# Attention probabilities leave two PSUM banks together: one instruction per engine and row, and waits per key block

## The reference

```
logits = einsum("bhqd,bhkd->bhqk", q, k) + causal + pos_bias
probs  = softmax(logits / 64)
out    = einsum("bhqk,bhkd->bhqd", probs, v)
x = x + layernorm(out_of_all_heads @ Wo + bo)
x = x + layernorm(moe(layernorm(x)))
```

## The kernel before

| slot | scores of row | transposes of row | fillers |
|---|---|---|---|
| 6 | 6 | 4 | values of the far half, key blocks 6 and 7 |
| 7 | 7 | 5 | values of the near half, block 0; the output projection in two pieces |
| 0 | 0 | 6 | values, near half, block 1; a q/k projection |
| 1 | 1 | 7 | values, near half, blocks 2 and 3; a q/k projection |
| 2 | 2 | 0 | none |
| 3 | 3 | 1 | values, far half, blocks 0 to 2; the output projection |
| 4, 5 | 4, 5 | 2, 3 | values, far half, block 3; then blocks 4 and 5 |

## Time and profile before

### The profile page before, as it was taken

The page is one execution under the profiler, slowest core; times in us unless marked ns, Lnnn a source line. Parts: engine busy times, 40 slices in busy tenths (PEclk is TensorE's granted clock), DMA queues, the critical chain, the costliest instruction groups (busy, mean ns, idle before and its releaser), DMA issues.

```text
span 858.1 us, 17060 instructions
## 1 busy us (share of the span) xinstructions
PE 770.3 (90%) x4436; PEld 656.1 (76%) x4436; DVE 712.8 (83%) x1596; ACT 612.1 (71%) x1340; POOL 298.6 (35%) x323
## 2 busy tenths in 40 slices
PE   3877999999999999999999999998469999999992
PEld 2657888888888888888888888887357877777771
DVE  5567888888888888888888888887879789998976
ACT  2356877877787788778777877875457776676672
POOL 2228723323332333233233323322321444554423
PEclk9999999999999999999999999999679999999997
DMA  7783244324423432443244234330003111222101
GB/s 274 242 267 81 62 85 89 72 61 86 98 61 72 93 80 61 86 93 66 61 92 92 61 76 89 79 74 26 25 1 126 48 39 61 73 73 73 50 1 49
DMA packets 56025, 70.72 MB, mean 82 GB/s; under 512 B 36032, under 2 KB 45120, under 8 KB 52544
## 3 DMA queue, kind: packets, MB, share of 16 engines
q1 hardware_dynamic: 55712, 69.83, 32.3%
q10 hardware_dynamic: 288, 0.59, 0.3%
HBM read 27.36 MB, written 9.50 MB: 43 GB/s over the span
## 4 chain that ended last, share of the span: by engine, by line
PE 70%; DVE 10%; issue 7%; ACT 5%; POOL 4%; DMA 3%; ACTq 0%; POOLq 0%; DVEq 0%; SPq 0%
PE out_ps L1184 16%; PE trans_ps L1166 15%; PE score_ps L1151 12%; PE shared_ps L1196 6%; DVE pT_lo L854 3%; PE trans_ps L1067 3%; PE score_ps L1067 2%; PE score_ps L1069 2%; ACT pT_hi L663 2%; PE score_ps L1068 2%; PE trans_ps L1068 2%; PE trans_ps L1069 2%; DVE pT_lo L954 2%; PE shared_ps L1067 2%; PE shared_ps L1069 2%
## 5 line engine op out<-in xcount | busy, mean ns | idle before, releaser
L648 ACT ACTIVATE probs<-score_ps,row_min 128x128 f32<-128x128 f32 (+7 forms) x256 | 190.3, 743 | 53.6 <-DVE row_min L841 53.0
L663 ACT ACTIVATE pT_hi<-trans_ps 128x512 fp32r<-128x512 f32 (+3 forms) x384 | 185.8, 493 | 58.6 <-PE out_ps L1184 30.0
L854 DVE TENSOR_TENSOR pT_lo<-trans_ps,pT_hi 128x512 fp32r<-128x512 f32 (+3 forms) x384 | 201.7, 553 | 30.4 <-ACT pT_hi L663 29.0
L841 DVE CUSTOM_DVE_ANT_0 score_ps<-score_ps,bias 128x128 f32<-128x128 f32 (+7 forms) x256 | 194.2, 759 | 20.9 <-PE score_ps L1151 18.9
L1166 PE MATMUL trans_ps<-ident,probs 128*128 128x128 f32 x1152 | 190.2, 274 | 20.7 <-DVE pT_lo L854 19.7
L1151 PE MATMUL score_ps<-k_hl,q_hl 128*128 128x512 f32 (+2 forms) x768 | 182.4, 351 | 3.2 <-DMA k_hl<-k_hl 1.6
L469 POOL TENSOR_TENSOR acc<-acc,head_out 128x512 f32<-128x512 f32 x64 | 82.8, 1294 | 263.1 <-DVE head_out L872 262.9
L1166 PEld LDWEIGHTS trans_ps<-ident,probs 128*128 128x128 f32 x1152 | 136.9, 140 | 44.8 <-DVE pT_lo L854 28.0
L1184 PE MATMUL out_ps<-pT_hi,v_hl 128*128 128x512 f32 (+2 forms) x384 | 156.5, 409 | 1.1 <-DVE pT_lo L854 1.1
L954 DVE TENSOR_TENSOR pT_lo<-probs,pT_hi 128x512 fp32r<-128x512 f32 x144 | 133.0, 950 | 25.0 <-ACT pT_hi L721 15.0
L1151 PEld LDWEIGHTS score_ps<-k_hl,q_hl 128*128 128x128 f32 x768 | 134.4, 188 | 23.7 <-DMA k_hl<-k_hl 1.8
(11 more groups left out here) (122 smaller groups left out, 1160.2 us busy)
## 6 DMA issues: line engine op xcount, KB each, us to landing
q_hl<-k_hl SPq DMA_DIRECT2D x64, 256.0 KB, 3.6
k_hl<-k_hl SPq DMA_DIRECT2D x32, 512.0 KB, 4.2
v_scratch<-probs SPq DMA_DIRECT2D x16, 512.0 KB, 4.1
v_raw<-v_scratch SPq DMA_DIRECT2D x32, 256.0 KB, 4.6
bias_all<-gate_scratch SPq DMA_DIRECT2D x8, 1024.0 KB, 4.8
v_raw<-in_Wfc SPq DMA_DIRECT2D x8, 256.0 KB, 4.9
bias<-in_Wproj SPq DMA_DIRECT2D x8, 256.0 KB, 5.3
bias_all<-in_rel_steps SPq DMA_DIRECT2D x1, 1920.0 KB, 12.8
```

The costliest lines, as they stand in the source:

```text
L648: act.activation(probs[s % 4][:, 0:n], scores_of(s % QB)[:, 0:n], ACT.Exp, bias=row_min[:, s:s + 1], scale=-1.0, accum_out=row_sum[:, s:s ...
L663: act.activation(pT_hi[c][:, CH * g:CH * g + m, q * P:(q + 1) * P], trans_ps[k % 2][:, 0:m * P].rearrange("p (m q) -> p m q", q=P), ACT.Co ...
L841: dve.tensor_tensor_reduce(out=ps, in0=ps, in1=bias_b[b][:, T - n:T], scale=1.0, scalar=3e38, op0=ALU.add, op1=ALU.min, accum_out=row_min[ ...
L854: dve.tensor_tensor(pT_lo[c][dst], trans_ps[k % 2][:, 0:m * P].rearrange("p (m q) -> p m q", q=P), pT_hi[c][dst], ALU.subtract).then_inc(p ...
```

## The change

`trans_ps` becomes two halves of one tile of 1024 columns over two banks. Rows of up to four blocks use bank i % 2. Rows of five blocks or more use both banks, and leave them in one instruction on ACT and one on DVE. `pT_psum`, `pT_hi_ready` and `pT_ready` now count rows (256), not groups (384). PE waits at a row's first group: for row 0 and rows 4 to 7 until all rows before are out; for rows 2 and 3 until the row two before is; for row 1 nothing more. The near half's wait on `oT_psum` stays. The far half's is split: its rows 4, 5 and 6 wait on a new semaphore `far_used`, which `values` raises after key blocks 3, 4, 5 and 6, and row 7 waits on `oT_psum`. The other edits write `trans_ps[r]` for `trans_ps[r][:]`.

```
+    def banks_of(i):
+        return [i % 2] if i < CH else [0, 1]
...
-        trans_ps = [pb(f"trans_ps{r}", [P, W]) for r in range(2)]
+        trans_wide = pb("trans_wide", [P, 2 * W])
+        trans_ps = [trans_wide[:, r * W:(r + 1) * W] for r in range(2)]
...
 split_hi (ACT)
-                if q == 0 and not (isinstance(u, int) and u < NC):
+                used = not (isinstance(u, int) and u < NC)
+                if c == 0 and q == 0 and used:
                     act.wait_ge(oT_psum, u - (NC - 1))
-                for g in range(GROUPS[i]):
-                    k = group_of(s, g)
-                    m = min(CH, i + 1 - CH * g)
-                    act.wait_ge(pT_psum, h * G_HEAD + k + 1)
-                    act.activation(pT_hi[c][:, CH * g:CH * g + m, q * P:(q + 1) * P],
-                                   trans_ps[k % 2][:, 0:m * P].rearrange("p (m q) -> p m q", q=P),
-                                   ACT.Copy).then_inc(pT_hi_ready, 1)
+                if c and used and q == CH - 1:
+                    act.wait_ge(oT_psum, u - (NC - 1))
+                elif c and used:
+                    act.wait_ge(far_used, (h * B + b - 1) * CH + q + 2)
+                act.wait_ge(pT_psum, h * S + s + 1)
+                at = banks_of(i)[0] * W
+                act.activation(pT_hi[c][:, 0:i + 1, q * P:(q + 1) * P],
+                               trans_wide[:, at:at + (i + 1) * P].rearrange("p (m q) -> p m q", q=P),
+                               ACT.Copy).then_inc(pT_hi_ready, 1)
...
 split_lo (DVE)
-                for g in range(GROUPS[i]):
-                    ...
-                    dve.wait_ge(pT_hi_ready, h * G_HEAD + k + 1)
-                    dve.tensor_tensor(pT_lo[c][dst], trans_ps[k % 2][:, 0:m * P]...
+                dve.wait_ge(pT_hi_ready, h * S + s + 1)
+                dve.tensor_tensor(pT_lo[c][dst], trans_wide[:, at:at + (i + 1) * P]...
...
 transpose_probs (PE)
                 if g == 0:
                     pe.wait_ge(probs_ready, h * S + s + 1)
-                if not (isinstance(h, int) and h == 0 and k < 2):
-                    pe.wait_ge(pT_ready, h * G_HEAD + k - 1)
+                    if i == 0 or i >= CH:
+                        if not (isinstance(h, int) and h == 0 and s == 0):
+                            pe.wait_ge(pT_ready, h * S + s)
+                    elif i > 1:
+                        pe.wait_ge(pT_ready, h * S + s - 1)
+                bank = banks_of(i)[g]
...
-                last.then_inc(pT_psum, 1)
+                if g == len(banks_of(i)) - 1:
+                    last.then_inc(pT_psum, 1)
...
 values (PE)
+                    if c and CH - 1 <= j < nk - 1:
+                        last.then_inc(far_used, 1)
```

More of the change, by code:

```diff
@@ L256, in transformer_block @@
         oT_psum = sem("oT_psum")
+        far_used = sem("far_used")
         oT_ready = sem("oT_ready")
@@ L602, in nT_evac @@
                 act.wait_ge(nT_psum, n * NCH + c + 1)
-                act.activation(nT_hi[:, c * W:(c + 1) * W], trans_ps[c % 2][:], ACT.Copy)\
+                act.activation(nT_hi[:, c * W:(c + 1) * W], trans_ps[c % 2], ACT.Copy)\
                    .then_inc(nT_hi_ready, 1)
@@ L791, in nT_evac @@
                 dve.wait_ge(nT_hi_ready, n * NCH + c + 1)
-                dve.tensor_tensor(nT_lo[:, c * W:(c + 1) * W], trans_ps[c % 2][:],
+                dve.tensor_tensor(nT_lo[:, c * W:(c + 1) * W], trans_ps[c % 2],
                                   nT_hi[:, c * W:(c + 1) * W], ALU.subtract).then_inc(nT_ready, 1)
@@ L848, in split_lo @@
                 c, q = divmod(i, CH)
-                for g in range(GROUPS[i]):
-                    k = group_of(s, g)
-                    m = min(CH, i + 1 - CH * g)
-                    dst = (slice(None), slice(CH * g, CH * g + m), slice(q * P, (q + 1) * P))
-                    dve.wait_ge(pT_hi_ready, h * G_HEAD + k + 1)
-                    dve.tensor_tensor(pT_lo[c][dst], trans_ps[k % 2][:, 0:m * P].rearrange("p (m q) -> p m q", q=P),
-                                      pT_hi[c][dst], ALU.subtract).then_inc(pT_ready, 1)
+                dst = (slice(None), slice(0, i + 1), slice(q * P, (q + 1) * P))
+                at = banks_of(i)[0] * W
+                dve.wait_ge(pT_hi_ready, h * S + s + 1)
+                dve.tensor_tensor(pT_lo[c][dst], trans_wide[:, at:at + (i + 1) * P].rearrange("p (m q) -> p m q", q=P),
+                                  pT_hi[c][dst], ALU.subtract).then_inc(pT_ready, 1)
             def invert_sums(h, b, c, j0, j1):
@@ L961, in gate_expert @@
                 if isinstance(e, int) and e == 0:
-                    dve.tensor_scalar(acc_T[:, cols], trans_ps[c % 2][:], bias, None, ALU.add)\
+                    dve.tensor_scalar(acc_T[:, cols], trans_ps[c % 2], bias, None, ALU.add)\
                        .then_inc(gated_ready, 1)
@@ L969, in gate_expert @@
                 dve.sem_inc(dve_passed, 1)
-                dve.scalar_tensor_tensor(out=gated[c % 2][:], in0=trans_ps[c % 2][:], scalar=bias,
+                dve.scalar_tensor_tensor(out=gated[c % 2][:], in0=trans_ps[c % 2], scalar=bias,
                                          in1=gate_rows[i][:, cols], op0=ALU.add, op1=ALU.mult)\
@@ L1158, in transpose_probs @@
                 i = s % QB
-                k = group_of(s, g)
                 if g == 0:
                     pe.wait_ge(probs_ready, h * S + s + 1)
-                if not (isinstance(h, int) and h == 0 and k < 2):
-                    pe.wait_ge(pT_ready, h * G_HEAD + k - 1)
+                    if i == 0 or i >= CH:
[4 more added lines that the diff above has]
+                bank = banks_of(i)[g]
                 for j in range(CH * g, min(CH * (g + 1), i + 1)):
                     o = (j - CH * g) * P
-                    last = pe.transpose(trans_ps[k % 2][:, o:o + P], probs[s % 4][:, j * P:(j + 1) * P], ident[:])
-                last.then_inc(pT_psum, 1)
+                    last = pe.transpose(trans_ps[bank][:, o:o + P], probs[s % 4][:, j * P:(j + 1) * P], ident[:])
+                if g == len(banks_of(i)) - 1:
+                    last.then_inc(pT_psum, 1)
             def values(h, b, c, j0, j1):
@@ L1173, in values @@
                 if j0 == 0:
-                    pe.wait_ge(pT_ready, h * G_HEAD + group_of(QB * b + CH * c + CH - 1, c) + 1)
+                    pe.wait_ge(pT_ready, h * S + QB * b + CH * c + CH)
                     if c == 0:
@@ L1225, in slot @@
                 if s >= LAG_PE or carried:
-                    for g in range(GROUPS[t % QB]):
+                    for g in range(len(banks_of(t % QB))):
                         transpose_probs(n, t, g)
@@ L1244, in _ @@
                 if s - LAG_PE < S:
-                    for g in range(GROUPS[(s - LAG_PE) % QB]):
+                    for g in range(len(banks_of((s - LAG_PE) % QB))):
                         transpose_probs(H - 1, s - LAG_PE, g)
@@ L1281, in second_layer @@
                 for k in range(HB):
-                    last = three(trans_ps[c % 2][:], wproj_hi[i][:, k, :], wproj_lo[i][:, k, :],
+                    last = three(trans_ps[c % 2], wproj_hi[i][:, k, :], wproj_lo[i][:, k, :],
                                  hidden_hi[c % 2][k], hidden_lo[c % 2][k], start=k == 0, stop=k == HB - 1)
```

## The result

The changed kernel takes **987.36 us** (985.56 to 988.69, 4 runs), the kernel before 861.41 (860.6 to 862.1). The ratio is 1.146 with a 95% interval of 1.1435 to 1.1487: slower by 126 us, where 118 were forecast. The profiled execution took 985.56 us over a span of 983.8, which is 125.6 more than the profiled execution before.

What follows compares the result with a forecast made beforehand. PE was taken to bound the kernel; losing the second buffer adds 3.70 us per unit, 118 us over 32 units, to the profiled 859.9, and with 1.1 for the median gives 979 us, range 950 to 1000.

Steps and rivals of the forecast that it cites:

- What bounds: Attention units: PE bounds, busy 16.2 of 16.8 us a unit, with one 0.56 us gap ahead of row 5's transposes.
- The three unguarded places: Ahead of the transposes of rows 6, 7 and the next row 0: no PE gap before the change; the ones to watch.
- The merged instructions: One ACT copy and one DVE subtraction per long row: 128 fewer on each engine, worth nothing on the path alone.
- The line through two forms: Merged instruction times from the 128 and 512 column forms: 105 ns per key block on ACT, 135 on DVE.
- bound on this price: Merged instructions' price per unit: 0.8 us less or 0.5 us more than the line, giving 953 to 996 us.
- The single buffer: PE's T0 of rows 5, 6, 7 and 0 waits for the whole row before: 3.70 us more per unit, 118 us.
- Row 4's new wait for row 3: Ahead of row 4's T0, PE must also wait for row 3 to leave; costed at nothing.
- the hand-over of 0.04 us from DVE to PE: From DVE's end to PE's next transposes: 0.04 us, part of 0.17 us of hand-overs per trip.
- row 4's gain of 0.04: After row 4's trip of 1.70 us, row 5's T0 would start at 318.72 instead of 318.76, 0.04 us earlier.
- The clock rival: Granted clock falls to 1.2 GHz from row 5 to row 0: 1104 us, chance 0.05; few units, near 1000, 0.03.
- hidden trips, faster: Trips of rows 5 to 7 fit behind PE's work, only row 5's wait counts: 19 us gained, 842 us, chance 0.02.
- What would show it: Profile signs: PE gaps ahead of rows 5, 6, 7, 0 of about 0.5, 1.0, 1.5, 1.2 us; wait some 130 us.

Runs made afterwards that it cites:

- e2_row_wait: Kernel before plus the waits per key block and PE's wait for the whole row before; instructions stay in pairs: 876.69 us, ratio 1.019.
- e4_act_merged: e1_block_wait with ACT's copy merged to one per row, DVE's subtractions in pairs, PE waiting by group: 932.17 us, ratio 1.083.
- e3_dve_merged: e2_row_wait with DVE's subtraction merged to one per row, ACT's copies still in pairs: 928.87 us, ratio 1.079.
- e1_block_wait: Kernel before with the far half's waits per key block alone; groups, banks and pairs of instructions stay: 843.38 us, ratio 0.980.
- e7_waits_swapped: Changed kernel with PE's two waits ahead of T0 exchanged, first pT_ready, then probs_ready: 982.01 us, ratio 1.140.

## Why the prediction was right

The sign, the place and the mechanism were as forecast, and 987.36 lies within 950 to 1000. Point by point:

- *What bounds.* The three unguarded places were the right ones to watch. All gained a gap.
- *The merged instructions.* The line through two forms held within 1% for all four lengths. Groups by form (count, busy us, mean ns, idle before):

```profile
L851 DVE TENSOR_TENSOR pT_lo<-trans_wide,pT_hi 128x1024 fp32r<-128x1024 f32 x32 | 39.2, 1225 | 52.1 <-ACT pT_hi L662 52.1
...
L662 ACT ACTIVATE pT_hi<-trans_wide 128x1024 fp32r<-128x1024 f32 x32 | 32.9, 1027 | 58.9 <-PE trans_wide L1166 58.9
```

  1.027 and 1.225 us against 1.022 and 1.230. Neither bound on this price (953 and 996) was needed. The Trainium skill, page "VectorE: DVE Perf Modes", section "The TRN2 errata — SBUF-src ops pay a fixed extra latency per instruction", was right about a fixed part per instruction, but the 20 us estimated from it did not show: the subtractions' own busy time fell by 8.0 us (201.7 to 193.7 by the two pages) and all of DVE's by 1.4. The pairs had already overlapped.
- *The single buffer.* Intervals forecast from rows 4, 5, 6 and 7: 2.64, 3.28, 3.52 and 3.77 us. Measured in the two units above: 2.78, 3.27, 3.56, 3.78 and 2.78, 3.34, 3.60, 3.83. Behind row 0 there were 7.28 us, where 7.2 and 0.06 for the late start were forecast. Row 4's new wait for row 3 cost nothing, as forecast: no gap stands ahead of it. The forecast did not single out that the merges, more than PE's wait, take the second buffer away; e2_row_wait and e4_act_merged show it.
- *The term that was mis-sized: the hand-over of 0.04 us from DVE to PE.* I took it from the one place where the trace of before had it. In the changed kernel's chain it is mostly 0.14. It also turned row 4's gain of 0.04 into a loss of 0.10. The long kind goes with the merged subtraction. From 150 to 560 us, all 25 hand-overs that PE waited for in the kernel before took about 0.06 us from DVE's end, and so did all 72 in e2_row_wait and all 85 in e4_act_merged, where DVE still subtracts in two halves. With one subtraction per row 75 of 86 in e3_dve_merged and 69 of 79 in the changed kernel took about 0.15. Why is not shown. At 0.09 us, three and a half times a unit, that is 10 us in 32 units, an estimate. Part of it was hidden by luck: the hand-over from PE to ACT, taken as 0.11, is only 0.08 behind rows 4 and 5, and 0.02 behind rows 6 and 7. The chain behind row 4's T1, which ends at 331.88:

```profile
331.88 0.02 issue
331.90 0.02 ACTq L660
331.92 0.04 issue
331.96 0.71 ACT pT_hi L662
```

  Per unit the average is 20.75 us against 20.51 forecast (16.81 and 3.70), 0.24 more, or 7.4 us over 31 units.
- *The clock rival came true in one place.* In the last unit the granted clock falls. Stretches of the changed kernel, and the transposes behind its three longest gaps in this part:

```profile
690.00:705.00 15.00, 11.02 (x74) 9.59 (x73) 8.94 (x22) 8.06 (x19) 2.58 (x2) 1.00 0.06 17
705.00:712.70 7.70, 5.21 (x36) 4.12 (x34) 4.69 (x8) 5.00 (x8) 1.40 (x2) 1.00 0.27 70
712.80:715.00 2.20, 1.05 (x5) 1.08 (x6) 1.00 (x1) 0.00 (x0) 0.20 (x1) 0.50 0.00 0
715.00:720.00 5.00, 3.42 (x13) 2.84 (x12) 2.92 (x11) 1.51 (x2) 0.00 (x0) 0.50 0.00 0
```
```profile
693.44 0.63 PE L1166 MATMUL trans_wide<-ident,probs 128*128 128x128 f32 x4 [2.05 <-DVE pT_lo L851]
...
697.28 0.30 PE L1166 MATMUL trans_wide<-ident,probs 128*128 128x128 f32 x1 [1.93 <-DVE pT_lo L851]
...
713.95 1.94 PE L1166 MATMUL trans_wide<-ident,probs 128*128 128x128 f32 x8 [1.93 <-DVE pT_lo L851]
```

  It goes from 2.4 to 1.2 GHz at 712.8 us, inside the gap of 1.93 us ahead of the last row 7, when PE had been idle for 0.7 us. The length of one gap does not tell when: the gaps of 2.05 and 1.93 us shortly before left the clock at 1.00, and so did those of up to 1.35 us from 100 to 690 us. The forecast named a granted clock under 1.00 in attention as a sign of being wrong; it shows, but only in the last 3 us of the transposes, where row 7's eight take 1.94 us instead of the 1.07 of the earlier trace rows. The last transposes begin 122.6 us later than before (715.5 against 592.9), and the rest of the 125.6, 3.0 us, falls behind them. There the first 7.1 us run at 0.50, and before the change they ran at 1.00; how much of the 3.0 us that is was not separated.
- *The rival "hidden trips, faster", 842 us*, was refuted for this change. Its gain is real, though: e1_block_wait takes it, 843.4 us, by leaving the merges out. The Trainium skill, page "TensorE: Matmul & The Clock Gate", section "HAM oscillation — how this bites in real kernels", reports no further gain from PSUM double-buffering in its kernel. Here e4_act_merged, which gives up little else, costs 89 us.
- *What would show it.* The gap ahead of row 5 was forecast at 0.5 and is 0.63; the others at 1.0, 1.5 and 1.2 and are 0.8, 1.3 and 1.2. A gap is counted from the modelled end of the last matmul, which can lie later than the next one's start would put it, and that may be why two are smaller. For the same reason, as I read it, PE's busy time rose from 770 to 788 us, which I had said would stay: the tail of a matmul that used to overlap the next one now stands alone ahead of each gap. The total wait was forecast at some 130 us. The list of waits has 112.1, but all idle time ahead of the transposes is 129.7:

```profile
L1166 PE MATMUL trans_wide<-ident,probs 128*128 128x128 f32 x1152 | 193.5, 277 | 129.7 <-DVE pT_lo L851 112.1 <-ACT probs L644 17.6
```

  The other 17.6 us are put down to an exponential on ACT, 20 times. In 19 of these DVE's subtraction had ended 0.15 us before PE went on, just as in front of rows 5, 7 and 0. At 357.68 us, ahead of row 6, the exponential named is that of row 7, which these transposes don't read. So they belong to the same wait.

## What to carry to other kernels

An instruction that reads two PSUM banks makes one buffer of them: before merging evacuations, count what the producer can do between its last write and its next first write, and set it against the full trip through every engine behind it. Two instructions that start half a row apart can be far better than one, even on engines with time to spare, and what the merge saves should be read from how much a pair takes together, not from two single durations. When a change has two parts, cost and try each alone: here one part is worth 17 us, and the other hides it and loses 144 against it.

## What was not expected of the hardware

PE's start after DVE's end comes in two kinds, about 0.06 and about 0.15 us, in the changed kernel with the weight load ahead of the matmul by 0.03 us in the second. The long kind shows where DVE subtracts a whole row at once and not where it subtracts in halves, and the order in which two waits are written shifts how many are of which kind (10 of 79 against 30 of 80 short).

The granted clock of the changed kernel held at 1.00 from 30 to 712.7 us, through units with four gaps of up to 1.35 us each and through two gaps of about 2 us near the end. e7_waits_swapped has two such gaps as well, 1.96 us ahead of 690.35 and 1.84 ahead of 694.12, and there the clock fell for a while behind them, although PE was then busy throughout:

```profile
690.00:695.50 5.50, 3.31 (x22) 2.76 (x23) 3.09 (x8) 2.92 (x8) 0.00 (x0) 1.00 0.00 0
695.60:698.90 3.30, 3.30 (x14) 2.91 (x13) 0.63 (x4) 0.84 (x3) 0.00 (x0) 0.50 0.00 0
```

Nearly the same gaps kept the clock in one kernel and lost it in the other; what decides is not shown.
